# A decoder layer in fp32 on one core: another order of all engines at an iteration's begin, the recurrence from one difference, and the third normalisation on ScalarE

## The reference, cut to what matters

```
x = layernorm(x + attention(x))          # 16 heads of 32, causal, with biases
x = layernorm(x + wkv(k=x, v=ctx))       # a recurrence over the tokens, per channel
x = layernorm(x + ffn(x))                # attention with one key and one value head,
                                         # picked per token by a gate
# the recurrence, w = -exp(time_decay), u = time_first:
ww = u + k_t; q = max(pp, ww); e1 = exp(pp - q); e2 = exp(ww - q)
y_t = (e1 * aa + e2 * v_t) / (e1 * bb + e2)
q2 = max(pp + w, k_t); e1 = exp(pp + w - q2); e2 = exp(k_t - q2)
aa, bb, pp = e1 * aa + e2 * v_t, e1 * bb + e2, q2
```

## Time and profile before

| | |
|---|---|
| median of 3 runs | 1825.88 us (1825.39 to 1827.17) |
| the profiled execution, its span | 1823.16 us, 1821.6 us |
| busy: PE, DVE, ACT, POOL | 1506.1, 1192.3, 575.3, 519.5 us (83, 65, 32, 29% of the span) |
| mean granted clock of TensorE | 0.924 |
| chain that ended last | PE 49%, DVE 28%, issue 11%, DMA 4%, ACT 3%, POOL 3% |

### The profile page before, as it was taken

The page is one execution under the profiler, slowest core; times in us unless marked ns, Lnnn a source line. Parts: engine busy times, 40 slices in busy tenths (PEclk is TensorE's granted clock), DMA queues, the critical chain, the costliest instruction groups (busy, mean ns, idle before and its releaser), DMA issues.

```text
span 1821.6 us, 29982 instructions
## 1 busy us (share of the span) xinstructions
PE 1506.1 (83%) x9792; PEld 1181.8 (65%) x9792; DVE 1192.3 (65%) x2423; ACT 575.3 (32%) x1296; POOL 519.5 (29%) x701
## 2 busy tenths in 40 slices
PE   4667888889898888979798898989889897988746
PEld 4445666767676676766677676667767666776433
DVE  3346585757758585776858576685857768585754
ACT  2223242423324332332423233242323323242312
POOL 1024150422415142240504233051423305141330
PEclk8668999999899998999999998999999998999979
DMA  5223232221323222132322213232221323222010
GB/s 139 87 62 79 53 74 74 65 67 44 81 52 83 68 66 59 44 81 52 87 64 64 61 44 81 52 87 64 67 58 44 83 51 87 64 67 60 21 46 13
DMA packets 63282, 118.24 MB, mean 65 GB/s; under 512 B 14480, under 2 KB 32912, under 8 KB 63248
## 3 DMA queue, kind: packets, MB, share of 16 engines
q1 hardware_dynamic: 63248, 117.80, 25.5%
HBM read 32.81 MB, written 8.39 MB: 23 GB/s over the span
## 4 chain that ended last, share of the span: by engine, by line
PE 49%; DVE 28%; issue 11%; DMA 4%; ACT 3%; POOL 3%; SPq 1%; DVEq 1%; ACTq 0%; POOLq 0%
PE pp L399 10%; PE pp L400 9%; PE pp L401 9%; DVE neg_max L1116 4%; PE po L495 3%; DMA q_stack<-max_rows 3%; PE sq L443 3%; PE po L509 2%; PE sq L422 2%; DVE w_val L1292 2%; DVE o_tok L1141 2%; DVE w_max L1196 2%; DVE stats L1147 2%; DVE w_max L1169 2%; PE po L499 2%
## 5 line engine op out<-in xcount | busy, mean ns | idle before, releaser
L856 ACT ACTIVATE prob<-sk 128x512 f32<-128x512 f32 x384 | 215.6, 596 | 446.5 <-PE sk L422 446.3
L1116 DVE TENSOR_REDUCE neg_max<-sq 128x2 f32<-128x512 f32 (+1 forms) x384 | 249.9, 678 | 50.9 <-PE sq L422 44.7
L399 PE MATMUL pp<-xt_hi,w_hi 128*128 128x256 f32 x768 | 233.1, 303 | 30.8 <-DVE w_lo L1103 14.3
L400 PE MATMUL pp<-xt_lo,w_hi 128*128 128x256 f32 x768 | 221.4, 288 | 0.0
L401 PE MATMUL pp<-xt_hi,w_lo 128*128 128x256 f32 x768 | 220.9, 288 | 0.0
L399 PE MATMUL pp<-w_hi,xt_hi 128*128 128x512 f32 x384 | 169.5, 442 | 26.2 <-DVE w_val L1292 21.9
L399 PEld LDWEIGHTS pp<-xt_hi,w_hi 128*128 128x128 f32 x768 | 151.9, 198 | 38.8 <-issue 22.5
L1140 DVE RECIPROCAL o_rec<-po 128x8 f32<-128x8 f32 x128 | 25.9, 202 | 204.1 <-PE po L509 204.0
L400 PE MATMUL pp<-w_lo,xt_hi 128*128 128x512 f32 x384 | 159.1, 414 | 0.0
L1517 POOL TENSOR_TENSOR xt_lo<-x_raw,xt_hi 128x1024 fp32r<-128x1024 f32 x16 | 38.0, 2375 | 422.0 <-ACT xt_hi L922 422.0
L401 PE MATMUL pp<-w_hi,xt_lo 128*128 128x512 f32 x384 | 157.3, 410 | 0.0
(11 more groups left out here) (155 smaller groups left out, 3556.3 us busy)
## 6 DMA issues: line engine op xcount, KB each, us to landing
q_stack<-q_hi SPq DMA_DIRECT2D x256, 128.0 KB, 2.3
q_stack<-q_lo SPq DMA_DIRECT2D x128, 128.0 KB, 2.3
k_stack<-k_hi SPq DMA_DIRECT2D x128, 128.0 KB, 2.3
x_raw<-in_xT SPq DMA_DIRECT2D x16, 512.0 KB, 3.6
k_stack<-k_lo SPq DMA_DIRECT2D x64, 128.0 KB, 2.3
xa<-in_x SPq DMA_DIRECT2D x16, 512.0 KB, 3.5
w_val<-in_ctxT SPq DMA_DIRECT2D x64, 128.0 KB, 2.1
out_y<-xb SPq DMA_DIRECT2D x16, 512.0 KB, 2.9
```

Source lines behind the costliest of these rows:

```text
L399: T.matmul(out, lh, rh, start=(c == 0), stop=False, skip_group_check=True)
L400: T.matmul(out, lh, rl, start=False, stop=False, skip_group_check=True)
L856: A.activation(dst, sk[n % 2][:], ACT.Exp, scale=SCALE).then_inc(s_exp, 1)
L1116: V.tensor_reduce(dst, src, AX.X, ALU.max, negate=True).then_inc(s_max, 1)
```

## The change

Five things are done.

1. The recurrence is computed from one difference, delta = k_t - (w_max of the token before + w), with `w_d[0]` set to 1e38. ScalarE forms Relu(-delta), Relu(delta) and Relu(now_cap - delta), then Exp(-x) of the first two (the two carry weights) and later Exp(60 - x) of the third (the weight of the current token, relative to the carried maximum). VectorE's clamps, its subtraction L1174, GpSimd's `difference` and two of its five products are gone.
2. The third normalisation is an Identity activation on ScalarE, with scale `rstd` and a bias that GpSimd computes (`third_bias`); it stands before the rows of group 1, and `store` is the first entry of SyncE's iteration.
3. TensorE transposes the maxima of groups 1 and 2 in the middle of a projection (`middle`), and the y transposes stand before the values of group 0. x2 is transposed before the out transpose of group 0.
4. VectorE takes all maxima of group 1 before the last division, and the second residual and its statistics before the normalisation of group 0. At the iteration's end, `k_lo` is computed before a third residual, and the last recurrence start before the division of chunk 1.
5. The DMAs of `k_hi` into the first group of `k_stack` wait for ScalarE's `k_hi` only, and that of `k_lo` comes behind them.

```
@@ SyncE
             def k_stacks(b, groups):
                 if groups[0] == 0:
-                    wait(sp, pa_free, PA_JOBS * b + PA_K + 2)
+                    wait(sp, pa_hi, 4 * b + PA_K + 2)
...
                 for g in groups:
-                    for lo, src in ((0, k_hi), (HD, k_lo), (2 * HD, k_hi)):
-                        stack(k_stack, lo, src, g, a_stk[g])
+                    stack(k_stack, 0, k_hi, g, a_stk[g])
+                    stack(k_stack, 2 * HD, k_hi, g, a_stk[g])
+                    if g == 0:
+                        wait(sp, pa_free, PA_JOBS * b + PA_K + 2)
+                    stack(k_stack, HD, k_lo, g, a_stk[g])
...
             def iteration(t, do_a, prev, nxt):
                 b = t - 1
+                if prev and not (isinstance(t, int) and t < 2):
+                    store(t - 2)
                 if do_a:
                     max_a(t, 1)
...
-                if prev and not (isinstance(t, int) and t < 2):
-                    store(t - 2)
@@ TensorE
                 for c in range(CC):
+                    if middle is not None and c == CC // 2:
+                        middle()
...
-                    project_a(t, PA_V + 1)
-                    max_a(t, 1)
+                    project_a(t, PA_V + 1, lambda: max_a(t, 1))
+                if prev:
+                    y_transpose(b, 1)
...
                     values_a(t, 0)
-                if prev:
-                    y_transpose(b, 1)
...
+                if prev:
+                    x2_transpose(b)
+                if do_a:
                     out_transpose(t, 0, a_free, A_JOBS * t + A_OT[0])
                     sq_a(t, 2, 2)
...
-                if prev:
-                    project_f(b, PF_Q)
+                if prev:
+                    project_f(b, PF_Q, (lambda: max_a(t, 2)) if do_a else None)
@@ ScalarE
             def carry_exps(b, c):
...
+                A.activation(w_e2[:, i, 1:S + 1], w_d[:, i, :], ACT.Relu, scale=-1.0)
+                A.activation(w_e1[:, i, :], w_d[:, i, :], ACT.Relu)
+                A.activation(w_d[:, i, :], w_d[:, i, :], ACT.Relu, scale=-1.0, bias=now_cap[:, c:c + 1])\
+                    .then_inc(w_relu, 1)
+                act.wait_ge(w_relu, CC * b + c + 1)
+                A.activation(w_e2[:, i, 1:S + 1], w_e2[:, i, 1:S + 1], ACT.Exp, scale=-1.0).then_inc(w_first, 1)
+                A.activation(w_e1[:, i, :], w_e1[:, i, :], ACT.Exp, scale=-1.0).then_inc(w_carry, 1)
...
+            def third_norm(b):
+                act.wait_ge(ln_biased, b + 1)
+                for c in range(TT):
+                    e = A.activation(xb[:, c, :], xb[:, c, :], ACT.Identity, scale=rstd[:, 2, c:c + 1],
+                                     bias=ln_bias[:, c:c + 1])
+                e.then_inc(x3_ready, 1)
@@ VectorE
+                V.memset(w_d[:, i, 0:1], -START_MAX)
                 dve.wait_ge(w_pp, CC * b + c + 1)
-                ch.mark(V.scalar_tensor_tensor(w_d[:, i, :], k, first[:, c:c + 1], w_max[:, i, 0:S],
-                                               ALU.add, ALU.subtract))
-                e2 = V.tensor_tensor(w_e2[:, i, 1:S + 1], k, w_max[:, i, 1:S + 1], ALU.subtract)
...
-                ch.link(V.tensor_scalar(w_key[:, i, :], w_d[:, i, :], -1.0, 0.0, ALU.mult, ALU.min))
-                V.tensor_scalar(w_d[:, i, :], w_d[:, i, :], 0.0, None, ALU.min).then_inc(w_min, 1)
+                delta = V.scalar_tensor_tensor(w_d[:, i, 1:S], k[:, 1:S], decay[:, c:c + 1], w_max[:, i, 1:S],
+                                               ALU.subtract, ALU.subtract)
@@ GpSimd
+            def third_bias(b):
+                G.tensor_tensor(neg_mean, meanvar[:, 2, :, 0], minus_one, ALU.mult).then_inc(pool_ln[2], 1)
...
+                G.tensor_tensor(ln_bias, neg_mean, rstd[:, 2, :], ALU.mult).then_inc(ln_biased, 1)
...
-                ch.mark(G.tensor_tensor(w_e1[:, i, :], w_key[:, i, :], w_max[:, i, after], ALU.mult))
+                G.tensor_tensor(w_key[:, i, :], w_e2[:, i, after], w_d[:, i, :], ALU.add).then_inc(w_den, 1)
                 ch.mark(G.tensor_tensor(w_ev[:, i, :], w_d[:, i, :], w_val[:, i, :], ALU.mult))
-                ch.mark(G.tensor_tensor(w_key[:, i, :], w_key[:, i, :], w_e2[:, i, after], ALU.mult))
                 ch.wait()
-                G.tensor_tensor(w_key[:, i, :], w_key[:, i, :], w_d[:, i, :], ALU.add).then_inc(w_den, 1)
-                G.tensor_tensor(w_ev[:, i, :], w_e1[:, i, :], w_ev[:, i, :], ALU.add).then_inc(w_den, 1)
+                G.tensor_tensor(w_ev[:, i, :], w_max[:, i, after], w_ev[:, i, :], ALU.add).then_inc(w_den, 1)
...
                 products(t, 2)
+                products(t, 3)
                 if prev:
                     inverse_std(t - 1, 2)
-                products(t, 3)
+                    third_bias(t - 1)
```

More of the change, by code:

```diff
@@ L394, in _, with products @@
         def _(pe):
-            def products(out, lhs, rhs):
+            def products(out, lhs, rhs, middle=None):
                 for c in range(CC):
+                    if middle is not None and c == CC // 2:
+                        middle()
                     (lh, ll), (rh, rl) = lhs(c), rhs(c)
@@ L408, in tokens, with channels_out, tokens_out @@
                 return lambda c: (hi_t[:, c, lo:lo + n], lo_t[:, c, lo:lo + n])
-            def channels_out(w, pair):
+            def channels_out(w, pair, middle=None):
                 for i in range(2):
+                    if middle is not None and i == 1:
+                        middle()
                     mm = products(pp[:, S * i:S * (i + 1)], weight(w, P * (2 * pair + i), P), tokens(0, S))
                 return mm
-            def tokens_out(bank, w, c, hi_t=xt_hi, lo_t=xt_lo):
-                return products(bank[:, 0:D], tokens(P * c, P, hi_t, lo_t), weight(w, 0, D))
+            def tokens_out(bank, w, c, hi_t=xt_hi, lo_t=xt_lo, middle=None):
+                return products(bank[:, 0:D], tokens(P * c, P, hi_t, lo_t), weight(w, 0, D), middle)
             def mask(out, tile, heads):
@@ L582, in project_a, with project_f @@
                 mm.then_inc(pa_job, 1)
-            def project_f(b, job):
+            def project_f(b, job, middle=None):
                 if job == PF_Q:
@@ L591, in project_f @@
                 if job < PF_K:
-                    mm = channels_out(W_FQ, job - PF_Q)
+                    mm = channels_out(W_FQ, job - PF_Q, middle)
                 elif job < PF_V:
@@ L682, in iteration @@
                 if do_a:
+                    out_transpose(t, 0, a_free, A_JOBS * t + A_OT[0])
+                    sq_a(t, 2, 2)
                     values_a(t, 1)
-                    max_a(t, 2)
+                    if not prev:
+                        max_a(t, 2)
                 if prev:
-                    project_f(b, PF_Q)
+                    project_f(b, PF_Q, (lambda: max_a(t, 2)) if do_a else None)
                 if do_a:
@@ L901, in carry_exps @@
             def carry_exps(b, c):
-                act.wait_ge(w_diff, CC * b + c + 1)
-                A.activation(w_e1[:, c % HC, :], w_e1[:, c % HC, :], ACT.Exp, bias=decay[:, c:c + 1])
-                if c % HC == 0:
+                i = c % HC
+                if i == 0:
                     act.wait_ge(w_even, HC * b + c // HC + 1)
@@ L908, in carry_exps @@
                     act.wait_ge(w_free, W_JOBS * b + W_X1J + c // HC + 1)
[L909 removed]
+                A.activation(w_e2[:, i, 1:S + 1], w_d[:, i, :], ACT.Relu, scale=-1.0)
[5 more added lines that the diff above has]
+                A.activation(w_e1[:, i, :], w_e1[:, i, :], ACT.Exp, scale=-1.0).then_inc(w_carry, 1)
             def now_exps(b, c):
[L913 to L915 removed]
+                A.activation(w_d[:, c % HC, :], w_d[:, c % HC, :], ACT.Exp, scale=-1.0, bias=now_high[:, 0:1])\
+                    .then_inc(w_now, 1)
             def x_split_hi(b):
@@ L956, in iteration @@
                     exps_a(t, 0, 2)
+                if prev and not (isinstance(t, int) and t < 2):
+                    third_norm(t - 2)
+                if do_a:
+                    row_hi_a(t, 1)
                     value_out(t, 1)
-                    row_hi_a(t, 1)
                     copy_a(t, 0)
@@ L1325, in iteration @@
                 if do_a:
-                    maxima_a(t, 1, 2)
                     rows_a(t, 1)
-                if prev and not (isinstance(t, int) and t < 2):
-                    ln_apply(2, t - 2, xb, xb, x3_ready)
+                if prev:
+                    second_residual(b, 1)
+                    second_stats(chy, b)
+                    chy.close()
                 if do_a:
@@ L1484, in _ @@
             dve.wait_ge(act_once, 2)
+            V.tensor_tensor(now_cap[:], first[:], decay[:], ALU.add).then_inc(dve_once, 1)
+            dve.wait_ge(dve_once, 2)
+            V.tensor_scalar(now_cap[:], now_cap[:], -1.0, NOW_HIGH, ALU.mult, ALU.add).then_inc(dve_once, 1)
             for job in range(PA_V):
@@ L1519, in _ @@
```

(8 more changed lines are left out.)

117 lines of the change are left out of this document (54 added, 63 removed).

## The result

The changed kernel took 1743.92 us (median of 4 runs, 1739.41 to 1746.85); the kernel before, on the same chip, 1825.64. The ratio is 0.9556, with a 95% interval of 0.954 to 0.9572: faster by 82 us. The forecast was 1751 us.

The account below looks back on a forecast made before the run. TensorE's own work fills almost all its time; waits, with VectorE behind them, and slow clock can be won. 15 periods x (1.3 + 1.5 + 1.2) = 60, plus 3 once and 12 of clock: 1751 us, range 1722 to 1805.

Parts of the forecast that it names:

- The clock: All periods: fewer slow stretches as waits go, half of 1.6 us taken, 0.8 us per period, 12 us in all.
- C: Last iteration: GpSimd's chain behind TensorE's 13.33 us wait loses products and a normalisation, 3 us once (1.4 to 4).
- A: Period's end: the first score matmul's wait for the k_stack DMA goes, net 1.3 us per period, A1 included.
- A1: Period's end: five ScalarE activations ahead of the softmax make TensorE's third sk tile late, a loss of 1.0 us.
- B1: Iteration's begin: group 1's maxima come first, their rows land before they are asked for, 1.5 us per period (0.8 to 1.9).
- it stays the same 1.3 ahead: From the new period's start to the third sq tile, VectorE is the chain and stays 1.3 us ahead.
- The y wait: Iteration's begin: TensorE's y transposes wait 0.3 us for the quotient behind VectorE's later division.
- B2: Iteration's begin: x2 is transposed 3.4 us sooner, group 2's rows take back 2.2, leaving 1.2 us per period (0 to 3.4).
- the slower rival: SyncE's store, first in the queue, holds up rows beyond 1.8 us of slack; 1847 us at 7.2 us late, chance 0.05.
- The rule on relu: Relu belongs on VectorE; as a rival, ScalarE's eight extra activations are a plain loss, 1841 us, chance 0.03.
- Half: ScalarE's delay eats the period-end gain, group 2's rows eat the x2 gain; 25 us remain, 1800 us, chance 0.22.
- the clock giving back more: Rival: less slow clock wins another 1.9 us per period, 1722 us, chance 0.15.

Follow-up runs that it names:

- e1: Changed kernel with the key stacks' DMAs in the old order behind k_lo, and the second projection's k_lo behind the third residual again; 1766.2 us.
- e4: Changed kernel with ScalarE's five activations of the recurrence's block 0 behind the first two softmax tiles of F's group 2; 1769.4 us.
- e10: Changed kernel with group 2's maxima transposed behind the first 6 products of projection Q, and clamps of blocks 0 and 1 on VectorE; 1718.5 us.
- e6: Changed kernel with the third normalisation back on VectorE and its store behind the last key stack on SyncE's queue; 1775.9 us.
- e8: Changed kernel with only the store back behind the last key stack on SyncE's queue, third normalisation left on ScalarE; 1768.8 us.
- e5: Changed kernel with the transposes of group 2's maxima behind the first 6 products of projection Q, not the first 12; 1727.2 us.

## Why the prediction was right, and where it was not

The time was right within 0.4%, and the order of the steps too. Of the split, the waits were near: 4.0 us per period forecast, 3.82 came. The clock was too small: 0.8 forecast, 1.57 came (1.70 in stage 2, less 0.13 in stage 3). That the total came within some 3 us of the 75 forecast for the profiled execution (78.3 of span) is partly luck: the clock gave some 11 us more, while the waits, the fifteenth period of the sum and C gave some 8 less.

- **A, 1.3 us.** Right: the `k_stack` wait went, stage 4 gave 1.50, and e1 gives 1.71 for that stage. A1 = 1.0 was measured as a wait of 0.94. What the prediction didn't see is that the order tried doesn't bring A1 back (e4), while moving the clamps does (e10).
- **B1, 1.5 us.** Right in kind, too large as a term: stage 1 gave 0.98. The words "it stays the same 1.3 ahead" came true, as the third `sq` tile is at 12.4 us in both kernels. Missed was what comes behind that tile. TensorE, at full clock from the period's start, came to it earlier and waited 1.83 us where it had waited 1.13. In the part behind it the clock is at 0.77 in six periods, where it had been at 0.80 in four. With a full clock there, stage 1 takes 18.4 us and took 19.7, so 1.3 was won; a slow one costs 1.0 to 1.3 again. The y wait (0.3 forecast) was 0.48.
- **B2, 1.2 us.** Its waiting share was right, 1.34, with x2 21.7 us after the start (21.5 forecast) and a wait for the rows of 1.07 (1.6 forecast). I had walked one of the four periods whose stage 2 ran at 1.00; the mean of all 14 was 14.04 us, not 12.63.
- **The clock, 0.8 us.** The mis-sized term. Half of 1.6 was a guess, and the kind that I walked was no clean kind: the earlier trace rows gives it 90.40 us of busy time at 0.97, and the period after 87.57 at 1.00. Its own slow stretch, though, lay in the first 12.3 us (10.96 us of busy time, 8.49 after), where it cost nothing.
- **The third normalisation and the store.** No wait of TensorE came from the normalisation on ScalarE, as said, and it's 7 us cheaper there than on VectorE (e6 against e8). The store's early place was the slower rival, with 1.8 us of slack; it went at 961.78, with the rows behind it at 963.32, and TensorE never waited for those. The same place was worth 25 us (e8), and the forecast had no term for it.
- **C, 3 us.** Too large. The y wait of the last iteration fell from 13.33 to 10.61, but from the last period's start to the end only 0.9 was won. Where the rest went stays open.

```profile
1663.82 1.12 PE L562 MATMUL pw<-ident,w_y 128*128 128x128 f32 x4 [10.61 <-POOL w_y L1576]
```

- **The rule on relu.** The Trainium skill ("ScalarE: Activation LUTs", Rules for kernel authors) puts relu, min and max on VectorE. As a rival, that the Relus are a plain loss, it fell. As advice it held for two blocks of four: with `max_a(2)` moved in both, 1718.5 against 1727.2. For all four, no difference was measured.
- **Half, and the clock giving back more.** "The rows of group 2 eat B2" did happen (1.07 us, and e5 wins 0.68 of it back), but B2's sum already had it, and neither A nor B2 was eaten. The rival that had the clock give more, 1722, had the right cause and too large a share: 2.7 us per period, where 1.57 came.

Where the clock falls, the windows tell in part. Before the change it was slow in the first 12.3 us of all 14 periods. Right behind the wait of 2.33 us for `k_stack`, and then in the same place with that wait gone:

```profile
992.47:996.50 4.03, 3.71 (x16) 0.55 0.85 209
```
```profile
948.39:952.40 4.01, 2.76 (x19) 1.00 0.85 212
```

With that wait put back (e1, 1.74 us), the first 12.3 us stand at 0.71 or 0.72 in seven periods and at 1.00 in seven. After the change four stand at 0.86, the first one at 0.67, and nine at 0.99 or 1.00. So the slow start of a period hung largely on the `k_stack` wait, though it cost no time there.

What stays open is why a wait brings a slow clock in one period and not in the next. Before the change, stage 2 ran at 1.00 in four periods and lower in ten, and the walked one of the four has waits of 1.70 and 1.04, where the one at 0.77 shown above has 1.70 and 0.87; after it, the same wait of 1.8 us in stage 1 has a slow clock behind it in six periods of 14. No run here tells them apart.

## What to carry to other kernels

Cut a steady loop at three or four marks and take busy time, idle time and granted clock of all its periods, before pricing anything from one walked period: the one walked here had its stage 2 at full clock, and ten of 14 did not. Then ask of each stretch which engine times its end. Busy time that TensorE saves ahead of a tile that VectorE times only becomes waiting (1.59 us per period here); a table of busy and idle time alone would book it as a gain. An order that makes a chain through several engines (residual, statistics, normalisation, transposes) start sooner was worth far more here than the instructions taken out of it, and the store that frees that chain's buffer belongs to it. A wait that one reorder removes can be a cover for another: try the order before counting it.
